# Layer-0 queries as seven Strassen products per pair of heads, made four slots ahead and kept in SBUF

## The reference, cut to what matters

```python
x = _rmsnorm(hidden_states, ln_weight)
h_q = (x @ w_q.T).reshape(b, lq, H, DH)          # 1024 tokens x 512 -> 32 heads of 128
h_k = (key_value_states @ w_k.T).reshape(b, lk, H, DH)
h_v = (key_value_states @ w_v.T).reshape(b, lk, H, DH)
score = jnp.einsum('bqhd,bkhd->bhqk', h_q, h_k) + position_bias[None]
score = jax.nn.softmax(jnp.where(m, score, -jnp.inf), axis=-1)
attn = jnp.einsum('bhqk,bkhd->bqhd', score, h_v).reshape(b, lq, H * DH)
out = attn @ w_out.T
return hidden_states + out
```

## Time and profile before

| | us |
|---|---|
| median of 3 runs (lowest to highest) | 1748.13 (1747.45 to 1748.26) |
| time of the profiled execution | 1748.51 |
| its span in the profile | 1746.3 |
| PE busy | 1695.1 (97% of the span) |
| DVE busy | 1188.1 (68%) |
| ACT busy | 892.4 (51%) |
| POOL busy | 557.3 (32%) |
| mean granted TensorE clock | 0.991 |

### The profile page before, as it was taken

How to read it: one execution, slowest core, us unless ns; L and a number is a source line. 1 busy time by engine, 2 the same in 40 slices (tenths; PEclk the granted TensorE clock), 3 DMA queues, 4 the chain that set the end, 5 groups by cost and what they waited for, 6 DMA issues and landing times.

```text
span 1746.3 us, 31656 instructions
## 1 busy us (share of the span) xinstructions
PE 1695.1 (97%) x10935; PEld 1529.8 (88%) x10935; DVE 1188.1 (68%) x2247; ACT 892.4 (51%) x2370; POOL 557.3 (32%) x535
## 2 busy tenths in 40 slices
PE   7999999999899999999997899999999999999998
PEld 6999999988899999999996688888888888888887
DVE  6444437556777777777767876767777777777676
ACT  4344344335454544545443266666666666666663
POOL 4222223201522222222223433333333333333343
PEclk9999999999999999999999999999999999999999
DMA  6444344444333333323322010111111111111001
GB/s 233 154 157 156 144 171 153 170 138 156 107 109 96 109 109 105 108 94 108 111 67 99 8 58 29 49 37 48 36 45 36 39 45 36 48 36 35 17 7 48
DMA packets 80590, 153.31 MB, mean 88 GB/s; under 512 B 6544, under 2 KB 58128, under 8 KB 76944
## 3 DMA queue, kind: packets, MB, share of 16 engines
q1 hardware_dynamic: 80528, 152.50, 25.9%
HBM read 108.43 MB, written 44.04 MB: 87 GB/s over the span
## 4 chain that ended last, share of the span: by engine, by line
PE 90%; DVE 5%; DMA 2%; ACT 1%; issue 1%; POOL 1%; SPq 0%; DVEq 0%; ACTq 0%; POOLq 0%
PE bank L1768 20%; PE bank L1720 18%; PE bank L1722 18%; PE bank L1721 18%; PE bank L1926 3%; PE bank L2076 3%; PE bank L1883 3%; PE bank L1871 2%; PE bank L2102 2%; PE bank L1974 1%; DMA vraw<-wv 1%; PE bank L2107 1%; DMA plain<-w 1%; PE bank L1737 1%; DVE vw_lo L1124 0%
## 5 line engine op out<-in xcount | busy, mean ns | idle before, releaser
L1720 PE MATMUL bank<-w_hi,xt_hi 128*128 (+2 forms) x512 | 178.5, 349 | 2.7 <-issue 1.2
L626 POOL TENSOR_TENSOR pr<-pr,rn 128x512 f32<-128x512 f32 x64 | 66.7, 1043 | 347.4 <-DVE rn L1354 347.4
L1722 PE MATMUL bank<-w_hi,xt_lo 128*128 (+2 forms) x512 | 173.4, 339 | 0.0
L685 POOL TENSOR_TENSOR p<-p,rn 128x512 f32<-128x512 f32 x128 | 133.3, 1042 | 121.9 <-DVE rn L1598 118.6
L1721 PE MATMUL bank<-w_lo,xt_hi 128*128 (+2 forms) x512 | 172.0, 336 | 0.0
L1720 PE MATMUL bank<-xt_hi,w0q_hi 128*128 128x256 f32 x512 | 149.8, 293 | 0.0
L1721 PE MATMUL bank<-xt_lo,w0q_hi 128*128 128x256 f32 x512 | 144.5, 282 | 0.0
L1006 ACT ACTIVATE p<-bank,nb,q_r 128x256 f32<-128x256 f32 x256 | 141.2, 562 | 6.3 <-DVE nb L1593 3.9
L1722 PE MATMUL bank<-xt_hi,w0q_lo 128*128 128x256 f32 x512 | 144.4, 282 | 0.0
L908 ACT ACTIVATE ptr<-bank 128x512 f32<-128x512 f32 x63 | 37.7, 598 | 188.1 <-PE bank L1871 188.1
L552 POOL TENSOR_TENSOR q_r<-q_ms,half 128x4 f32<-128x4 f32 x64 | 64.5, 1008 | 192.2 <-DVE q_ms L1573 192.2
(11 more groups left out here) (227 smaller groups left out, 5487.4 us busy)
## 6 DMA issues: line engine op xcount, KB each, us to landing
stage<-w SPq DMA_DIRECT2D x35, 512.0 KB, 3.2
keys_of_layer<-kout SPq DMA_DIRECT2D x16, 1024.0 KB, 4.3
values_of_layer<-vout SPq DMA_DIRECT2D x16, 1024.0 KB, 4.8
kt<-keys_of_layer SPq DMA_DIRECT2D x64, 256.0 KB, 3.0
vs<-values_of_layer SPq DMA_DIRECT2D x64, 256.0 KB, 2.8
vraw<-wv SPq DMA_DIRECT2D x12, 1024.0 KB, 6.8
kraw<-wk SPq DMA_DIRECT2D x16, 512.0 KB, 5.2
stage0q<-w SPq DMA_DIRECT2D x16, 512.0 KB, 4.0
```

The lines of the kernel that those rows point to most:

```text
L626: pool.tensor_tensor(by4(pr), by4(pr), rn[:, :].unsqueeze(2).to_broadcast([P, 4, P]), ALU.mult).then_inc(norm_done, 1)
L685: pool.tensor_tensor(p1[:, half_p:half_p + 2, :], p1[:, half_p:half_p + 2, :], rn1[:, half_p:half_p + 2].unsqueeze(2).to_broadcast([P, 2, ...
L1720: nc.tensor.matmul(out_ap, l_hi, r_hi, start=(c == 0), stop=False)
L1722: op = nc.tensor.matmul(out_ap, l_lo, r_hi, start=False, stop=(c == n - 1))
```

## The change

Query weights come in the quartered layout of the key weights (`wq0`). For groups n = 2 to 15, the queries of a pair of heads and all 1024 tokens are made by the seven products, spread over the four slots of the group before: products 1 and 2 in slot p = 0, 6 and 7 in p = 1, 5 in p = 2, 3 and 4 in p = 3, each 6 matmuls of 512 columns. ACT copies one partial result per slot and DVE adds one in p = 0, 2 and 3, into a new buffer `queries_of` with room for two groups; scores read the queries there. The weights of the next group are split in two parts (early 512 columns, late 1280 columns), after four sums on POOL in slot p = 2.

The queries of groups 0 and 1 are still made by `queries0`'s way (now `first_queries`), all in the first four slots: slot 0 makes one, slots 1 to 3 two each. In the same slots DVE makes the four token differences (three operations of 1024 columns each for T1 and T3, two for T2 and T4), ACT rounds them in slots 1 to 4 and DVE makes their low parts in slots 4 and 5. `dequantise` is now none in p = 0, one in p = 1 and 2, two in p = 3. The last four slots make no queries.

```diff
+            def load_query_weight(n):
+                sp.wait_ge(kw_lo_done, 2 * query_weight(n))
+                sp.dma_start(qraw[:, A22:, :, :], wq0[n, :, :, :, :]).then_inc(kraw_in, 16)
```

SP, in a slot:

```diff
-                if p in (1, 3) and not last:
-                    w = p // 2
-                    sp.wait_ge(w_lo_done[w], n + 2)
-                    load_weight(w, n + 2)
+                if p == 1 and not last and not (isinstance(t, int) and t == 0 and j == 1):
+                    load_query_weight(n + 2)
+                if p == 3 and not last:
+                    sp.wait_ge(w_lo_done[1], n + 2)
+                    load_weight(1, n + 2)
```

POOL, in a slot, behind `masked_bias`:

```diff
+                if j % 4 == 2 and not last:
+                    m = query_weight(2 * t + j // 4 + 2)
+                    weight_sums(qraw, kraw_in, ksum_done, m, m - 1)
```

ACT, in a slot:

```diff
                 exponentials(i + 1)
-                if not (first and j == 0) and not (last and j == BODY - 1):
-                    queries_out(i + 2)
+                if first and 1 <= j < 4:
+                    queries_out(2 * j + 1)
+                    queries_out(2 * j + 2)
+                if not (first and j < 4) and not (last and j >= 4):
+                    query_part(n + 1, 1 - parity, p)
                 if not (first and j == 0):
                     output_hi(i, j - 1)
...
+                if first and 1 <= j < 5:
+                    query_difference_hi(j - 1)
+                if p == 1 and not last:
+                    query_weight_early(n + 2)
...
+                if p == 3 and not last:
+                    query_weight_late(n + 2)
```

DVE, in a slot, behind `maxima` and `accumulate`:

```diff
+                if active and p == 0:
+                    query_weight_late_lo(n + 1)
+                if active and p == 3:
+                    quarter21_of_queries(n + 1, 1 - parity)
                 inverse_sums(i + 1, 2 * (j % 4))
                 if lag1:
                     output_lo(i, (j - 1) % 2)
...
+                if first and j < 4:
+                    query_difference(j)
+                if first and 4 <= j < 6:
+                    query_difference_lo((T2, T1)[j - 4], (9, 11)[j - 4])
+                    query_difference_lo((T3, T4)[j - 4], (10, 12)[j - 4])
+                if active and p == 0:
+                    quarter11_of_queries(n + 1, 1 - parity)
+                if active and p == 2:
+                    quarter22_of_queries(n + 1, 1 - parity)
+                if p == 1 and not last:
+                    query_weight_early_lo(n + 2)
...
-                dequantise(2 * t + j // 4, j % 4, i + 1)
+                if p in (1, 2):
+                    dequantise(n, p - 1, i)
+                if p == 3:
+                    dequantise(n, 2, i)
+                    dequantise(n, 3, i + 1)
...
+            def query_difference(d):
+                dst = raw_t(d)
+                if d in (T1, T3):
+                    one, other = ((0, 1), (0, 0)) if d == T1 else ((1, 1), (0, 1))
+                    link(nc.vector.tensor_tensor(dst, x_hi(*one), x_hi(*other), ALU.subtract))
+                    link(nc.vector.tensor_tensor(dst, dst, x_lo(*one), ALU.add))
+                    nc.vector.tensor_tensor(dst, dst, x_lo(*other), ALU.subtract).then_inc(diff_done, 1)
+                else:
+                    block_of, less = ((1, 1), T1) if d == T2 else ((1, 0), T2)
+                    dve.wait_ge(diff_done, 5 + less)
+                    link(nc.vector.tensor_tensor(dst, x_hi(*block_of), raw_t(less), ALU.subtract))
+                    nc.vector.tensor_tensor(dst, dst, x_lo(*block_of), ALU.add).then_inc(diff_done, 1)
```

PE:

```diff
+            def query_product(number, which, start):
+                a, x_hi, x_lo = QUERY_BLOCKS[number]
+                for c in range(2):
+                    for l, r in ((qw_hi, x_hi), (qw_hi, x_lo), (qw_lo, x_hi)):
+                        op = nc.tensor.matmul(bank[which][:, :], l[:, a, c, :], r[:, c, :], start=start, stop=False, skip_group_check=True)
+                        start = False
+                op.then_inc(product_done, 1)
...
-                if not (last and j == BODY - 1):
-                    queries0(t + (j + 1) // BODY, (j + 1) % BODY)
+                if first and j < 4:
+                    for k in QUERIES_IN_SLOT[j]:
+                        first_queries(k)
+                elif not (last and j >= 4):
+                    query_products(n + 1, p)
```

More of the change, by code:

```diff
@@ L78, in build @@
             kvc = place.enter_context(nc.sbuf_tensor("keys_values_of_context", [P, 2, 256], fp32))
+        with ExitStack() as place:
+            qt_t_hi = place.enter_context(nc.sbuf_tensor("qt_t_hi", [P, 4, 2, 512], fp32r))
+            with ExitStack() as same:
+                qt_t_raw = same.enter_context(nc.sbuf_tensor("qt_t_raw", [P, 4, 2, 512], fp32))
+            qt_t_lo = place.enter_context(nc.sbuf_tensor("qt_t_lo", [P, 4, 2, 512], fp32r))
         ct_hi = keep("ct_hi", [P, C, B * P], fp32r)
@@ L485, in _ @@
             sp.dma_start(fbias[:, :], ffn0_bias.to_broadcast([P, D])).then_inc(fbias_in, 16)
-            for piece, used, count in ((2, w_lo_done[1], NG), (0, q_ps, U - 4), (1, y_ps, U - 4), (3, added, U), (4, s_ps, U)):
+            for piece, used, count in ((2, w_lo_done[1], NG), (0, s_ps, U), (1, y_ps, U - 4), (3, added, U), (4, s_ps, U)):
                 sp.wait_ge(used, count)
@@ L925, in slot @@
                 exponentials(i + 1)
-                if not (first and j == 0) and not (last and j == BODY - 1):
-                    queries_out(i + 2)
+                if first and 1 <= j < 4:
[3 more added lines that the diff above has]
+                    query_part(n + 1, 1 - parity, p)
                 if not (first and j == 0):
                     output_hi(i, j - 1)
-                if p in (0, 2) and not (last and j >= 4):
-                    w = p // 2
-                    act.wait_ge(w_in[w], 16 * (n + 2))
-                    wait(act, (q_ps, y_ps)[w], 4 * n)
-                    nc.scalar.activation(w0_hi[w][1 - parity][:, :], stage0[w][:, :], ACT.Copy).then_inc(w_hi_done[w], 1)
+                if first and j == 0:
+                    act.wait_ge(w_in[0], 32)
+                    nc.scalar.activation(w0_hi[0][1][:, :], stage0[0][:, :], ACT.Copy).then_inc(w_hi_done[0], 1)
+                if first and 1 <= j < 5:
+                    query_difference_hi(j - 1)
+                if p == 1 and not last:
+                    query_weight_early(n + 2)
+                if p == 2 and not (last and j >= 4):
+                    act.wait_ge(w_in[1], 16 * (n + 2))
+                    wait(act, y_ps, 4 * n)
+                    nc.scalar.activation(w0_hi[1][1 - parity][:, :], stage0[1][:, :], ACT.Copy).then_inc(w_hi_done[1], 1)
+                if p == 3 and not last:
+                    query_weight_late(n + 2)
             for j in range(BODY):
@@ L1372, in slot @@
                 lag1 = not (first and j < 1)
+                active = not (first and j < 4) and not (last and j >= 4)
                 if first and j == 0:
@@ new lines, in query_product, with query_products @@
+            def query_product(number, which, start):
[5 more added lines that the diff above has]
+                op.then_inc(product_done, 1)
+            def query_products(n, p):
+                job = query_job(n)
+                first = isinstance(n, int) and n == 2
+                if p == 0:
+                    pe.wait_ge(kw_lo_done, 2 * query_weight(n) + 1)
+                    if first:
+                        pe.wait_ge(qt_done, 8)
+                    else:
+                        pe.wait_ge(c12_done, job)
+                    query_product(1, 0, True)
+                    pe.wait_ge(c11_done, job)
+                    query_product(2, 1, True)
+                if p == 1:
+                    pe.wait_ge(kw_lo_done, 2 * query_weight(n) + 2)
+                    if first:
+                        pe.wait_ge(t_lo_done, 10)
+                    pe.wait_ge(part1_done, job)
+                    query_product(6, 0, False)
+                    pe.wait_ge(c21_done, job)
+                    query_product(7, 2, True)
+                if p == 2:
+                    if first:
+                        pe.wait_ge(t_lo_done, 11)
+                    pe.wait_ge(part2_done, job)
+                    query_product(5, 0, False)
+                if p == 3:
+                    pe.wait_ge(part4_done, job)
+                    query_product(3, 0, False)
+                    if first:
+                        pe.wait_ge(t_lo_done, 12)
+                    pe.wait_ge(c22_done, job + 1)
+                    query_product(4, 2, False)
```

131 lines of the change are left out of this document (108 added, 23 removed).

## The result

The changed kernel takes 1772.57 us (median of 4 runs, 1770.97 to 1774.88) beside 1747.91 for the kernel before in the same comparison: 1.0142 of it, 95% interval 1.0125 to 1.016, or 24.7 us slower. The forecast was 1757 with a range of 1744 to 1768, so the direction was right and the size was not.

What follows compares the result with a forecast made beforehand. PE, busy 97% of the span, was taken to bound the kernel. First slots +18, steady groups -7.8, last slots -2.2 and end +1.2 gave +9.2 us on 1748.5, or 1757 after the 0.4 to the median; range 1744 to 1768.

Steps and rivals of the forecast that it cites:

- PE's gain: Seven products instead of four slots' queries save PE 1.62 us a group, 22.7 us over 14 groups at most.
- The first eight slots: Slots 0 to 7: DVE's differences delay scores; walked slot by slot to 20.5 us longer, taken as 18 (12 to 22).
- The hold-up itself: DVE's 1024-column operation on two SBUF inputs ends 1.08 us after the POOL operation it met.
- the sign that the forecast named: DVE differences of 2 us or more in slots 0 to 3; 1.3 us each would show the reasoning wrong.
- The price without hold-up: First eight slots without POOL and DVE delaying each other: 13 us longer than a kernel before also without it.
- The steady groups: Groups 1 to 13: each gains some 0.6 us (0.1 to 1.2), together 7.8 us (1.3 to 15.6).
- the delay into p = 2: Early split after the load, beside POOL's sums, makes slot p = 2 late by 0.5 us (0 to 1.2), paid in full.
- the lateness of p = 0 and p = 3: Scores 1.2 us late in p = 0 cost 0.1 us; about 1.1 late in p = 3, within the projection's cover.
- rival 1: Steady groups gain nothing, as late load and POOL's sums delay slot p = 2; 1763 us, chance 0.2.
- The slot is 6.73 instead of 6.38: In slot p = 2 the projection waits for accumulate to 3.88 us, so a group gains 1.27, not 1.62.
- The last four slots and the end: Last slots, bound by accumulate, gain 2.2 us (1 to 3.3); a second dequantise behind slot 63 costs 1.2 (0.6 to 2).
- so they delay nothing by themselves: POOL's four sums, 3.0 us a group, start behind masked bias in p = 1 and end before the reciprocal.

Runs made afterwards that it cites:

- e13: e9 with a separate signal for each of DVE's two adds and PE's projection waiting per bank; 3.6 us faster than the kernel before (0.998).
- e8: Kernel before plus only DVE's ten token-difference operations in slots 0 to 3, results unused; 11.3 us slower than the kernel before.
- e16: Changed kernel with POOL nearly silent in the first eight slots, most of its operations there on 8 columns; 17.5 us slower than the kernel before.
- e5: Changed kernel with the query weights' load issued one slot earlier, behind the values' load; 22.2 us slower than the kernel before.
- e2: Changed kernel with POOL's sums of query weights on 4 of 128 columns from group 3 on; 12.6 us slower than the kernel before.
- e9: e7 with the query weights' load ahead of the values' load in SP's stream; 5.1 us slower than the kernel before (1.0031).
- e4: Changed kernel with one dequantise in each slot, as before; 17.2 us slower than the kernel before.
- e7: Changed kernel with query weights' load one slot earlier, POOL's sums in slot p = 1, one dequantise per slot; 10.6 us slower than the kernel before.
- e3: Changed kernel with POOL's residual operations of slots 1 to 4 on 8 of 512 columns; 22.2 us slower than the kernel before.

## Why the prediction was right in direction and wrong in size

**PE's gain: right.** A pair of products makes a slot of 7.76 and product 5 one of 6.36 where nothing is late (e13): 3 x 7.76 + 6.36 = 29.64, 1.61 under the 31.25 of before, where 1.62 was forecast. e13 gets 1.48 of it.

**The first eight slots: the mechanism right, the term too small, 22.4 for 18.** The walk gave 20.5 and was cut to 18 because it ran 1.0 too long on the kernel before. That cut was one error. The other was that the walk left out the lower clock, which had hit one slot of before and hit three of after (0.86, 0.88, 0.74). That 20.5 is near 22.4 is partly luck, since two errors in it cancel. Slots 0 and 1, 3 and 5, at full clock or nearly so, were walked as 18.5, 15.1 and 9.3 and took 17.9, 13.8 and 8.2: the walk gave the three operations of a difference 6.2 and 6.0, and they took 4.6 and 5.1. Slots 2, 4 and 6, with the lower clock in them, were walked as 11.0, 11.7 and 10.7 and took 12.39, 12.71 and 13.12. In slot 6 PE's matmul of 512 columns takes 0.77 in place of 0.47, behind a wait of 4.5 us:

```profile
505.32 0.77 PE L1863 MATMUL bank<-w0o_hi,ot_hi 128*128 128x512 f32 x1 [4.52 <-DVE residual L1420]
```

The hold-up itself, 1.08 behind POOL's end, came out to the hundredth where a difference met `bm`. But the sign that the forecast named, differences of 2 us or more, did not appear: the ten took 1.21 to 1.68, between that and the 1.3 that was to refute it (in e8 three of them took 2.1 to 2.2). The price without hold-up was put at 13 for both kernels without it; e16's 76.8 - 63.4 = 13.4 is not that quantity, as its kernel before had its POOL as it was.

**The steady groups: wrong, a gain of 7.8 forecast and 2.1 lost in groups 2 to 13.** This is the step that failed, and the largest part of the miss: two of its terms, the delay into p = 2 and the lateness of p = 0 and p = 3, were too small, and a third was no bound of the work.
- The delay into slot p = 2 was taken as 0.5, the range 0 to 1.2. It was 0.47 to 0.49 (sc at 1.57 for 1.09) in six groups and 1.17 in six: at rival 1's value half of the time. The load's landing was counted as just in time at its median; the six late groups show that a step with no cover must be costed at the late half of its row. On average it was 0.8, 0.3 more than taken. Both causes are needed for the 1.17: without the late landing it is 0.48 (e5), and without the sums it is 0 in seven groups and at most 0.36 in the others (e2).
- Slot p = 0 was to be 0.1 late from two `dequantise` and p = 3 within its cover. They were 0.4 and 0.17: 8.17 and 7.93 for 7.76. At the end of p = 3 the first of the two `eq` met `bm` and took 1.43, which the walk of the steady slot had left out though the earlier trace rows showed it. It is harmless with one `dequantise` behind it: e9 still has the 1.44, and p = 0 takes 7.76. Together the two slots cost 0.5 more than taken.
- "The slot is 6.73 instead of 6.38" held for this kernel where nothing else is late (6.81 in e2 and e9), but it is no bound of the work, only of one signal for two adds (e13: 6.36).

The sum 1.27 - 0.1 - 0.5 = 0.6 becomes 1.62 - (7.60 - 6.38) - 0.4 - 0.17 = -0.17 with the measured slots (7.60 the mean of p = 2 in groups 2 to 13), as 31.25 - 31.43 = -0.18 says. Rival 1, nothing gained in the steady groups, was nearest to them; it missed 3.4 there (a gain of 1.3 for a loss of 2.1), the first slots' extra 4.4 and the 1.3 before slot 0.

The recorded sums have small slips of their own. 1.27 - 0.1 - 0.5 is 0.67 and not 0.6, and with a delay of 1.2 it is 0 and not 0.1. The 13 groups were counted as 1 to 13, but group 1 lies in the walk of the first eight slots, and group 14, which makes products too, is in no term; the count comes out the same. Rival 1's terms give 1764 and not 1763.

**The last four slots and the end.** The forecast was -2.2 for the slots: slots 60 to 62 took 8.06, 6.77 and 6.81, 1.8 less than 3 x 7.81. Group 14, without POOL's sums, took 30.69, 0.6 less than before. Behind slot 63 the second `dequantise` cost 1.4 for 1.2, and e4 took it back.

**The clause "so they delay nothing by themselves"** was wrong for the place where the sums stood: there they lengthened `eq` and `wl` by 0.4 each (e2: 0.7 a group). One slot earlier in POOL's stream they are free (e9).

The Trainium skill (page "SBUF — State Buffer", section "Who interferes with whom") says that a DVE instruction with two SBUF inputs contends with a GpSimd instruction that reads SBUF. The traces agree: the differences took up to 1.68 beside POOL and 1.21 to 1.25 where it was silent (e16). The same section of the Trainium skill says that a DVE instruction with at most one SBUF input contends only in a two-port mode, which `tensor_scalar` can enter. The traces fit that as well: in e9 a sum out of PSUM took 0.68 beside `bm`, and the `eq` behind it, a `tensor_scalar` with one SBUF input, 0.89, ending 0.29 behind `bm`, where alone it takes 0.53. In which mode that `eq` ran no run shows.

What stays open is the clock's own share of the 22.4. Length times (1 - clock) bounds what changed at 6.8 - 1.7 = 5.1. e7 and e9 differ in the place of one load and have 1.7 and 6.8 of it, with first slots of 83.9 and 86.0; that puts 5.1 of it at some 2 us (an estimate from one pair of executions). No run held the clock still.

## What to carry to other kernels

Cost DVE's and POOL's work by where it meets, not by its length: the same 3 us of POOL cost 0.7 a group in one slot and nothing in the slot before, once the load that they wait for stood one place earlier in SP's stream. When a change makes PE's slot shorter, look for the waits that are coarser than the data (one signal for two banks) before moving work; and what fills an engine's wait for another, as `accumulate` does, must stay there. A walk that gives 20.5 is to be forecast as 20.5, with the lower clock on top of it where the walk makes PE wait.

## What the runs showed of the hardware that was not expected

- In the first slots of the changed kernel, waits of PE of 3.15, 3.24 and 4.52 us stand just before or in the stretches at the lower clock (slots 2, 4 and 6), while one of 2.91 in slot 3 was followed by none. The length of the wait doesn't decide it: in slot 60 the changed kernel has waits of 0.69 and 1.92 and a clock of 1.00, and e5, with 0.69 and 1.93, has 0.82 and 1.4 us more. e2 and e3 have 0.82 in this slot too. So two kernels that differ by 2 us of work can be nearer or farther apart by one such stretch:

```profile
930.97 0.47 PE L1863 MATMUL bank<-w0o_hi,ot_hi 128*128 128x512 f32 x1 [1.92 <-DVE residual L1420]
926.68 0.77 PE L1863 MATMUL bank<-w0o_hi,ot_hi 128*128 128x512 f32 x1 [1.93 <-DVE residual L1420]
```

- ACT's early part starts 3.7 to 4.7 us after the issue of the load that it waits for, in otherwise equal groups, and these 1.0 us split them into two lengths, 31.1 and 31.8.
- POOL's residual operations on 8 columns of 512 still took 2.6 to 3.7 us for two in three of the four slots, beside DVE's differences (e3): a short operation that is held up takes about as long as the other engine's work, whatever its own length. Where no difference stood beside them, two took 0.67 to 0.68 (e16).
